# Relative-position products in one pass, queries moved by DMA, and a rearranged first image in a three-layer attention and expert kernel

## The reference, cut to what matters

```
# layer A, on each image
xn = layer_norm(x)                          # padded to 28 x 28, four windows of 14 x 14
q, k, v = xn @ qkv_w + qkv_b                # 12 heads of 16 channels
attn = q*scale @ k.T + rel_h + rel_w        # rel_h[y,x,ky] = q[y,x] . rel_pos_h[y-ky+13], rel_w alike by columns
x = x + softmax(attn) @ v @ proj_w + proj_b
x = x + gelu(layer_norm(x) @ fc1_w + fc1_b) @ fc2_w + fc2_b
# layer B, on each image: causal attention over its 256 tokens, 12 heads
x = x + softmax(causal(q @ k.T / 16)) @ v @ lin_w.T + lin_b
# layer C, on all 2048 tokens: 8 experts, the best two of each token
x = x + sum over 2 experts: gate * (gelu(ln(x) @ w1[e] + b1[e]) @ w2[e] + b2[e])
```

## Time and profile before

| what | value |
|---|---|
| three runs, median (lowest to highest) | 907.41 us (894.43 to 911.28) |
| profiled execution, device time | 902.76 us |
| its span in the trace | 900.5 us |
| PE busy | 775.0 us, 86% |
| DVE busy | 457.3 us, 51% |
| ACT busy | 334.8 us, 37% |
| POOL busy | 135.1 us, 15% |

### The profile page before, as it was taken

The page is one execution under the profiler, slowest core; times in us unless marked ns, Lnnn a source line. Parts: engine busy times, 40 slices in busy tenths (PEclk is TensorE's granted clock), DMA queues, the critical chain, the costliest instruction groups (busy, mean ns, idle before and its releaser), DMA issues.

```text
span 900.5 us, 15570 instructions
## 1 busy us (share of the span) xinstructions
PE 775.0 (86%) x5670; PEld 677.1 (75%) x5670; DVE 457.3 (51%) x1114; ACT 334.8 (37%) x724; POOL 135.1 (15%) x241
## 2 busy tenths in 40 slices
PE   5359989989988998998899899886868899999990
PEld 3347867877877886887688688675757899999990
DVE  3172465675765767356576756655354422222223
ACT  5103134443442442334145244233336344444430
POOL 5000000001201111020112102102121321212210
PEclk9965789998997997589699799869989799999996
DMA  7890762102102111010211120073832111111116
GB/s 223 215 223 10 168 160 80 38 18 75 55 23 70 46 37 56 25 52 20 72 46 36 36 75 25 28 211 98 256 80 83 55 41 41 46 41 40 42 36 218
DMA packets 56032, 72.16 MB, mean 80 GB/s; under 512 B 6371, under 2 KB 45119, under 8 KB 55703
## 3 DMA queue, kind: packets, MB, share of 16 engines
q1 hardware_dynamic: 52550, 64.17, 26.2%
q0 software_dynamic: 3408, 7.02, 2.3%
HBM read 27.26 MB, written 23.17 MB: 56 GB/s over the span
## 4 chain that ended last, share of the span: by engine, by line
PE 72%; DVE 16%; issue 3%; SPq 2%; DMA 2%; ACT 2%; POOL 2%; DVEq 0%; ACTq 0%; POOLq 0%
PE ps L2070 8%; PE ps L1727 7%; PE ps L1728 6%; PE ps L1769 6%; PE ps L2053 6%; PE ps L2054 6%; PE ps L1912 3%; PE ps L1813 3%; PE ps L1885 3%; DVE max_rows_a L1212 3%; PE ps L1851 3%; PE ps L1936 3%; PE ps L1837 3%; DVE den L1232 3%; PE ps L1732 2%
## 5 line engine op out<-in xcount | busy, mean ns | idle before, releaser
L2053 PE MATMUL ps<-rows_t,w_tile 97*128 97x128 f32 x468 | 91.1, 276 | 2.1 <-DVE rows_t L1442 2.1
L2054 PE MATMUL ps<-rows_t,w_tile 96*128 96x128 f32 x468 | 90.5, 274 | 0.0
L2070 PE MATMUL ps<-w_exp,hid_t 128*128 x468 | 85.0, 333 | 1.9 <-DVE y_out L1450 1.4
L1274 DVE TENSOR_REDUCE max_b<-ps 128x3 f32<-128x384 f32 x96 | 48.9, 550 | 68.7 <-PE ps L1953 67.4
L1769 PE MATMUL ps<-s_q,rel_w 128*128 128x96 f32 x512 | 80.3, 319 | 2.1 <-DMA s_q<-staged_a 1.1
L1433 DVE COPY w_tile<-w_exp 96x768 f32 x39 | 21.7, 556 | 114.6 <-PE ps L2054 112.9
L2070 PEld LDWEIGHTS ps<-w_exp,hid_t 128*128 128x128 f32 x468 | 76.9, 194 | 3.4 <-issue 3.3
L1769 PEld LDWEIGHTS ps<-s_q,rel_w 128*128 128x128 f32 x512 | 73.8, 207 | 3.1 <-DMA s_q<-staged_a 1.7
L839 ACT ACTIVATE probs_a<-ps 98x392 f32<-98x392 f32 x96 | 47.9, 499 | 75.2 <-PE ps L1840 72.9
L2053 PEld LDWEIGHTS ps<-rows_t,w_tile 97*128 97x128 f32 x468 | 72.9, 191 | 3.0 <-DVE rows_t L1442 3.0
L2054 PEld LDWEIGHTS ps<-rows_t,w_tile 96*128 96x128 f32 x468 | 71.0, 191 | 0.0
(11 more groups left out here) (224 smaller groups left out, 1676.0 us busy)
## 6 DMA issues: line engine op xcount, KB each, us to landing
xs_dram<-blank SPq DMA_DIRECT2D x32, 388.0 KB, 8.9
w_exp<-in_e_w SPq DMA_DIRECT2D x16, 576.0 KB
ks_a<-staged_a SPq DMA_DIRECT2D x32, 192.0 KB, 3.4
qs_b<-staged_b SPq DMA_DIRECT2D x32, 192.0 KB, 3.0
ks_b<-staged_b SPq DMA_DIRECT2D x32, 192.0 KB, 3.2
tile_x<-xs_dram SPq DMA_DIRECT2D x39, 97.0 KB, 1.9
w_exp<-y_dram SPq DMA_DIRECT2D x8, 384.0 KB, 5.8
rel_w<-in_rel_tables SPq DMA_DIRECT2D x1, 1792.0 KB, 9.6
```

Source lines behind the costliest of these rows:

```text
L1274: ins = dv.tensor_reduce(max_b3[:, h, :], BANK_C[:, h % 3, 0:384].rearrange("p (a k) -> p a k", a=3), AX.X, ALU.max, negate=True).then_inc ...
L2053: pe.matmul(dst, w1_tile[t % 2][:, 0, cols], rows_t[t % 2][:, 0, :], start=True, stop=False)
L2054: ins = pe.matmul(dst, w1_tile[t % 2][0:DC, 1, cols], rows_t[t % 2][0:DC, 1, :], start=False, stop=True)
L2070: ins = pe.matmul(TILE_Y[:, 0:D], hid_t[t % 2][:, f, :], w_exp[:, bass.ds(e, 1), 2 * MLP + f * D:2 * MLP + (f + 1) * D].rearrange("p e d - ...
```

## The change

- **Tables and products.** `rel_w` becomes fp32r with 64 columns instead of 128 fp32 columns; its rows hold high and low parts of the tables, and `s_q` holds high and low queries, each twice, so that one pass gives the exact sum. q no longer passes through it. The tables come in two transfers of 128-byte pieces into `rel_raw` and are split by ACT (`tables_high`) and DVE (`tables_low`).
- **Queries.** `queries_in_a` makes eight transfers of 96 KB instead of two, after the high part (ACT) and the low part (new, `low_queries_a` on DVE). New: POOL puts both into window order (`query_windows`), and `query_rows_in_a` moves them into `qs_a` by four transfers. `max_a(0)` waits for them too (`q_in_a`).
- **values_a and normalise_a.** Products write PSUM in image order, with the edge in two pieces (28 and 32 columns); `normalise_a` becomes the sequence of `normalise_b`; PE may write the bank again after its first transpose (`dn_a` for `ot_a`).
- **Counts** of the routing are bf16 products.
- **First image.** Norms and identity have a semaphore of their own; padded keys go straight from SBUF; loads of the network, routing and layer B weights move into step 0 behind first work; most of POOL's memsets come later; fills are spread over three images (`FILLED = 3`).
- **Order.** All `step` and `last` lists are new. Norms are cut in two (sums, then the rest).

The diff, cut to its core:

```diff
-            rel_w = sb("rel_w", [P, 2 * WS, P])
+            rel_w = sb("rel_w", [P, 2 * WS, SLOT], F32R)
-            s_q = sb("s_q", [P, PAIRS, TOK])
-            rel_sum = sb("rel_sum", [P, PAIRS, TOK])
+            s_q = sb("s_q", [P, PAIRS, TOK], F32R)
+            rel_sum = sb("rel_sum", [SLOT, PAIRS, TOK])
...
+            sp.wait_ge(blanked, 1)
             for dst, src in rel_loads:
                 sp.dma_start(dst, src).then_inc(rel_in, 16)
...
             def queries_in_a(i):
-                sp.wait_ge(qh_a, i + 1)
-                if i == 0:
-                    sp.wait_ge(rel_in, REL_IN)
-                for e in range(2):
-                    sp.dma_start(s_q[SLOT * e:SLOT * e + HD, :, :], staged_a[:, e, :]).then_inc(q_in_a, 16)
+                for low, ready in enumerate((qh_a, ql_a)):
+                    sp.wait_ge(ready, i + 1)
+                    for e in range(2):
+                        for part in range(2):
+                            first = SLOT * e + 2 * HD * part + HD * low
+                            sp.dma_start(s_q[first:first + HD, :, :].bitcast(F32), staged_a[:, 2 * low + e, :]
+                                         ).then_inc(s_in_a, 16)
+
+            def query_rows_in_a(i):
+                if i:
+                    sp.wait_ge(av_a, GROUPS * i)
+                for low, first in enumerate((HIGH, LOW)):
+                    sp.wait_ge(qw_a, 2 * i + low + 1)
+                    for twice in range(2):
+                        sp.dma_start(qs_a[first + twice:first + 2 * HD:2, :, :].bitcast(F32),
+                                     staged_a[:, 8 + 2 * low:10 + 2 * low, :]).then_inc(q_in_a, 16)
...
(SP's step)
+                for i in a:
+                    fill(0)(i)
+                    load_pads(i)
...
+                    keys_in_a(i)
...
+                for i in c:
+                    store_t2(i)
+                for i in a:
+                    query_rows_in_a(i)
...
(ACT)
+            def tables_high(i):
+
+                if i == 0:
+                    ac.wait_ge(rel_in, REL_IN)
+                    ac.copy(rel_w[:, :, :], rel_raw[:, :, :]).then_inc(tables_set, 1)
...
+                for i in a:
+                    tables_high(i)
...
+                for i in a:
+                    channels_a(i)
...
(DVE)
-                    dv.stream_shuffle(den[:, :], src, [HD] * 32).then_inc(dn_a, 1)
+                    dv.transpose(o_cols[:, :], BANK_Z[:, 0:TOK]).then_inc(dn_a, 1)
                     dv.wait_ge(dn_a, done)
-                    dv.reciprocal(den[:, :], den[:, :]).then_inc(rc_a, 1)
-                    dv.wait_ge(rc_a, done)
-                    for dst, val, d in zip(window_pieces(yx(o_a[:, g:g + 1, :])), win_order(src.unsqueeze(1)),
-                                           win_order(den[:, :].unsqueeze(1))):
-                        ins = dv.tensor_tensor(dst[:, 0], val[:, 0], d[:, 0], ALU.mult)
-                    ins.then_inc(ot_a, 1)
+                    after(dv.reciprocal(sums_a[:, :], blocks[:, :, HD]))
+                    after(dv.tensor_tensor(blocks[:, :, 0:HD + 1], blocks[:, :, 0:HD + 1],
+                                           sums_a[:, :].unsqueeze(2).to_broadcast([P, TOK // 32, HD + 1]),
+                                           ALU.mult))
+                    dv.transpose(o_a[:, g, :], o_cols[:, :]).then_inc(ot_a, 1)
...
(PE)
-                dst = bank[:, j * 96:(j + 1) * 96].rearrange("p (g x) -> p g x", g=PAIRS)
+                dst = bank[0:SLOT, j * 96:(j + 1) * 96].rearrange("p (g x) -> p g x", g=PAIRS)
                 return pe.matmul(dst, rel_w[:, table, :], toks, start=True, stop=True)
...
                     if p == 0:
                         pe.wait_ge(q_done, i + 1)
+                        pe.wait_ge(q_in_a, 64 * (i + 1))
                         pe.wait_ge(k_in_a, 64 * (i + 1))
...
-                        ins = pe.matmul(BANK_Z[r:r + 32, WIN:TOK], v_a[:, 2 + k, h, :],
-                                        probs_a[:, slot // 2 % 3, slot % 2, 2 * WIN + k * OUT:2 * WIN + (k + 1) * OUT],
+                        pe.matmul(z[1][r:r + 32], v_a[:, 2 + k, h, :],
+                                  probs_a[:, slot // 2 % 3, slot % 2, first:first + EDGE],
+                                  start=(k == 0), stop=(k == 1))
...
+                        ins = pe.matmul(z[2][r:r + 32], v_a[:, 2 + k, h, :],
+                                        probs_a[:, slot // 2 % 3, slot % 2, first + EDGE:first + OUT],
                                         start=(k == 0), stop=(k == 1))
```

775 lines of the change are left out of this document (458 added, 317 removed).

## The result

The changed kernel takes 829.25 us (median of four runs, 824.24 to 831.85) against 906.96 (894.43 to 911.28) for the kernel before: ratio 0.918, 95% interval 0.907 to 0.929. The forecast was 862, with 836 to 890 as its range: the direction was right, the size was not. In some executions of either kernel TensorE stays at the low clock level for longer, whatever the kernel; times are therefore medians of several executions, and a step's length is the median of one trace's steps.

The account below looks back on a forecast made before the run. PE's own work was taken to bound the step. Products with values_a -35, normalise_a -2, order -6, edge +8 and first image -7 sum to -42 from 902.76, so 861; the forecast was 862, range 836 to 890.

Parts of the forecast that it names:

- normalise_a: Shorter normalisation on DVE: counts only where PE waits at output_a, 1.5 us over six steps, perhaps 2 with early PSUM release.
- The products: Relative-position products in fp32r, one record each: 8.85 us an image becomes 2.9, saving 5.9 (5.0 to 7.0).
- The split of values_a: Edge part in pieces of 28 and 32 columns: costs 0 to 1.0 us an image, taken as 0.8.
- PE's own work sets the step: Typical full step: PE busy for 65.91 of 71.80 us, with 5.9 us of waits.
- the cover of the new low parts: New low queries and window copies cost nothing, covered by PE's attention work between q_a and rel_rows; uncovered some 2 us an image.
- Order: Reordered step: PE's waits for x_nb and xt_g get work in front, 6 of 10 us gained over six steps.
- the edge: Step's edge: max_a(0) waits for query transfers, 1.3 us late a step, +8 us in all (0 to 24).
- the order does more: Rival: all x_nb and xt_g waits and half the rest go, PE stays at high clock; 827 us, chance 0.07.
- The long step: The step of 84.20 us at granted clock 0.76: a lasting low-clock stretch costs about 12 us, already in the sum.
- The first image: Before the first max_a: the wait behind route_constants goes, max_a starts near 47 us; -7 us (-2 to -10).
- the range's dear end: First image's table load: lands again in 9.6 us if small pieces are dear, holding channels_a back by some 5 us.
- The end: Last stage and expert tiles: same work in another order, PE gapless; 0, within 3 us either way.

Follow-up runs that it names:

- e15: Changed kernel with four-pass fp32 position products and normalise_a's full-tile reciprocal again, leaving the new order and loads alone; 895.5 us, ratio 1.002 to the kernel before.
- e1: Changed kernel with the position products' operands rel_w and s_q declared fp32 again, so four passes; 868.4 us.
- e10: Changed kernel with normalise_a's reciprocal over the whole 128x256 tile again instead of 128x8; 868.1 us.
- e14: Kernel before with only the new values_a and normalise_a put in; 886.2 us, ratio 0.991.
- e13b: Kernel before with only the position products in one pass: tables and s_q rounded to fp32r, low parts left out; 884.7 us.
- e12: Kernel before with only the head of the step in the new order on PE and DVE; 893.8 us, ratio 0.999.
- e5: Changed kernel with only the head of each step, from the second on, in the old order on PE and DVE; 872.6 us.
- e3: Changed kernel with query rows ahead of store_t2 on SP, and a wait for their landing ahead of the late loads; 837.7 us.
- e7: Changed kernel with packed tables, query rows ahead of store_t2, and late loads and fills behind the transfer of image 0's maxima; 825.2 us.
- e2: Changed kernel with all engines in the old order from the second step on, query rows behind the key rows on SP; 925 us.
- e6: Changed kernel with all engines in the old order from the second step on, query rows at the end of SP's step; 911 us.
- e4: Changed kernel with position tables packed by the host, one transfer of 7 KB pieces instead of two of 128-byte pieces; 820.2 us.

## Why the prediction was wrong, point by point

**normalise_a.** This is the step that failed. The forecast gave it -2 us in all, 0.3 a step, since DVE has 24 us to spare in a step and so counts only where PE waits for it at output_a. In the new order the relief is worth 5.2 to 5.6 us a step (e15 to e1, e10 to after). The spare time is a share over stages with different limits; in the attention stage of the new order DVE's list is late, and PE stands for max_b and o_a and loses the clock behind them (e10). The five ordinary steps gained 51.9 us where the forecast had 26, and five times 5.2 us is about that difference. In the old order the forecast's size was nearly true (1.1, e14).

**The products.** The term was right: 5.9 forecast for the records, 9.7 - 3.4 = 6.3 measured (its base of 8.85 and its 2.9 were both read somewhat low); and of the 5.1 us a step that it made with values_a, 5.0 to 5.4 came in the new order (e15 to e10, e1 to after). The split of values_a was dearer in the forecast (0.8) than on the chip (28 and 32 columns take 0.41 us a group, before 0.33: 0.25 an image). But the argument, "PE's own work sets the step", holds only in the new order, which the forecast did not ask for; there the term is right by luck. Alone in the old order the passes save 2.1 (e13b). There the products were also the cover of a trip and of DVE's normalisation, and the forecast, which named the cover of the new low parts, did not ask what the shortened work itself covered.

**Order.** -6 over the steps by the forecast, +8 for the edge: together nothing, and by itself the new order gives nothing (73.0 against 72.7 us, e15; e12). What the forecast did not have is that the order decides whether the other two count: with both in place its head alone is worth 5.7 us a step (e5). It counted the waits for x_nb and xt_g, 10.4 us over six steps, and left out the longest ones, 13.6 us for DVE's row maxima, of which 3.6 are left.

The rival "the order does more" gave 827 at a chance of 0.07; its time was nearly met, but not by its mechanism: most of the waits went and the clock rose, and yet the order without the other two parts gives nothing (e15). **The edge** was right: 1.3 forecast, 1.5 measured, up to 1.6 when removed (e3, e7). **The long step** of before, 85.5 us at 0.76 (84.20 by the forecast's cuts, which lie behind the first products), did not come back, some 12 us beyond an ordinary step's gain; the forecast carried it over without a chance of its own. Whether that is luck stays open: of the six traces in the old order three have a step over 80 us (before, e2, e6) and three have none (e12, e13b, e14), and in the new order there is none, but no run tests why. **The first image** failed at the table load: the range's dear end was 5 us worse, and the load was dearer still, 12.1 us where both bounds were 2.4 and 9.6; undoing it gives back 6.3 (e4). **The end** was taken at 0 within 3, since the same work stood there in another order and PE was gapless; it cost 6.2, in the 29 tiles behind the first ten, where PE has gaps now.

## What to carry to other kernels

Judge the slack of an engine by the stage, not by its share of the step: an engine that is idle for a third of the step was the one that PE waited for in the middle of it. Before a shortened operation is booked as a gain, list what ran beside it and whether that is the next to be late. Ask for each saving in which order of the work it counts: here two savings gave 2.1 and 1.1 us alone, and 5 us and more each, added up, in the new order. And load many small pieces as few long ones, above all where an in-order engine has the next work queued behind them.

## What the runs showed of the hardware

A wait of 1 to 2 us by PE in the middle of dense work can be followed by a stretch at the low clock level: in e10's third stretch, behind waits of 2.1 and 1.3 us, the clock is 0.83 where the changed kernel has 1.00. It need not be: in a step of e15 the same wait of 2.1 us for max_b is followed by 1.00. And the low level can last long although PE has no pause, as for 30 us in the long step of before (PE busy for all of it at 0.50):

```profile
360.00:390.00 30.00, 30.00 (x196) 24.09 (x194) 10.40 (x21) 8.87 (x26) 0.00 (x0) 0.50 0.08 21
```

In fp32, 32 position products take nearly the same with 64 stationary columns as with 128 (9.1 and 9.7 us an image); in fp32r the columns tell, 3.4 us with 64 (after) and 4.6 with 128 (e13b). A reciprocal of 128x256 takes 1.75 us on DVE, of 128x8 0.20.
